# A transformer layer on one core: early maxima in pairs, bias stores spread over chunks, base rows per batch, and another order at the end

## What is computed

```python
B, S, _ = hidden_states.shape
qkv = jnp.transpose((xn @ W_qkv).reshape(B, S, 3, NUM_HEADS, HEAD_DIM), (0, 3, 2, 1, 4))
q, k, v = (qkv[:, :, 0], qkv[:, :, 1], qkv[:, :, 2])
scores = jnp.einsum('bhqd,bhkd->bhqk', q, k) + compute_bias(rel_emb, S, S)
attn = jax.nn.softmax(scores.astype(jnp.float32), axis=-1)
att = jnp.transpose(jnp.einsum('bhqk,bhkd->bhqd', attn, v), (0, 2, 1, 3)).reshape(B, S, EMBED_DIM) @ W_out
...
expert_out = jnp.matmul(jax.nn.gelu(jnp.matmul(xn, w1) + b1), w2) + b2
ffn = expert_out * jnp.sum(combine, axis=-1, keepdims=True)
return x + att + ffn
```

## Time and profile before

| | us |
|---|---|
| median of 3 runs | 3178.73 (3175.87 to 3179.97) |
| the profiled execution | 3177.1 |
| its span, first to last instruction | 3175.2 |
| first pass | 0 to 565 |
| attention, 64 heads | 567 to 3109 |
| projection and stores | 3109 to 3175.2 |

### The profile page before, as it was taken

One profiled execution on the slowest core, in us unless ns is written; L12 is line 12 of the kernel. 1 busy time (PEld: TensorE's weight loads), 2 busy tenths in 40 slices (PEclk: granted clock), 3 DMA queues, 4 the chain that ended last, 5 costly groups with the idle time before them and its releaser, 6 DMA issues.

```text
span 3175.2 us, 72323 instructions
## 1 busy us (share of the span) xinstructions
PE 3137.2 (99%) x28162; PEld 1780.7 (56%) x28162; DVE 2816.9 (89%) x3745; ACT 2437.5 (77%) x4665; POOL 1299.6 (41%) x1920
## 2 busy tenths in 40 slices
PE   7999999999999999999999999999999999999998
PEld 6988889544444444444444444444444444444447
DVE  5577765899999999999999999999999999999923
ACT  4444335688888888888888888888888888888893
POOL 1211212444444444444444444444444444444445
PEclk9999999999999999999999999999999999999999
DMA  8433224432222222222222222222222222222106
GB/s 199 120 93 87 80 80 115 74 68 37 38 38 37 38 38 37 38 38 38 38 37 38 37 38 38 38 38 38 37 38 38 38 38 38 38 38 37 24 9 191
DMA packets 135541, 174.37 MB, mean 55 GB/s; under 512 B 52913, under 2 KB 99633, under 8 KB 128865
## 3 DMA queue, kind: packets, MB, share of 16 engines
q1 hardware_dynamic: 135200, 169.75, 26.2%
HBM read 109.26 MB, written 56.69 MB: 52 GB/s over the span
## 4 chain that ended last, share of the span: by engine, by line
PE 80%; DMA 1%; POOL 0%; DVE 0%; SPq 0%; issue 0%; ACT 0%; DVEq 0%; POOLq 0%; ACTq 0%
PE ps L1153 38%; PE ps L1170 25%; PE ps L1175 9%; PE ps L1142 7%; DMA out_rows<-base_in 1%; PE ps L1209 0%; DVE max_half L1091 0%; DMA base_in<-base_rows 0%; POOL k_st L259 0%; POOL prob L1056 0%; POOL turned L1064 0%; ACT turned L1016 0%; DMA total_sb<-o_sb 0%; DMA recip_rows<-recip_all 0%; SPq L920 0%
## 5 line engine op out<-in xcount | busy, mean ns | idle before, releaser
L1091 DVE TENSOR_REDUCE max_half<-ps 128x1 f32<-128x512 f32 (+1 forms) x2666 | 2408.5, 945 | 35.9 <-PE ps L1142 27.0
L1009 ACT ACTIVATE prob<-ps 128x512 f32<-128x512 f32 x4096 | 2156.4, 600 | 360.2 <-PE ps L1153 356.8
L1056 POOL TENSOR_TENSOR prob<-prob,near 128x224 f32<-128x224 f32 (+2 forms) x1664 | 976.0, 601 | 1384.5 <-ACT prob L1009 1378.1
L1142 PE MATMUL ps<-k_st,q_st 48*128 48x512 f32 x3968 | 1485.5, 461 | 0.4 <-DVE max_half L1091 0.3
L1153 PE MATMUL ps<-q_st,k_st 49*128 49x512 f32 x4096 | 1347.3, 431 | 3.2 <-PEq L266 2.3
L1153 PEld LDWEIGHTS ps<-q_st,k_st 49*128 49x128 f32 x4096 | 661.8, 184 | 864.7 <-ACT prob L1009 728.6
L1170 PE MATMUL ps<-prob,vr 128*32 128x384 f32 x4864 | 757.0, 498 | 0.0
L1142 PEld LDWEIGHTS ps<-k_st,q_st 48*128 48x128 f32 x3968 | 640.7, 184 | 62.1 <-DVE max_half L1091 9.8
L1170 PE MATMUL ps<-prob,vx 128*32 128x384 f32 x3328 | 594.6, 500 | 2.4 <-POOL prob L1056 1.3
L728 PE MATMUL ps<-xnt,w_parts 128*128 128x512 f32 x1152 | 271.7, 395 | 7.7 <-DVE parts L569 4.3
L1175 PE MATMUL ps<-prob,vx 128*32 128x128 f32 x7040 | 276.0, 277 | 0.4 <-POOL prob L1056 0.4
(11 more groups left out here) (70 smaller groups left out, 1162.6 us busy)
## 6 DMA issues: line engine op xcount, KB each, us to landing
qk_parts<-parts SPq DMA_DIRECT2D x64, 512.0 KB, 4.5
q_st<-qk_parts SPq DMA_DIRECT2D x192, 128.0 KB, 3.8
k_st<-qk_parts SPq DMA_DIRECT2D x192, 128.0 KB, 5.5
near<-bias_near SPq DMA_DIRECT2D x64, 352.0 KB, 6.3
x_sb<-in_L_attn_hidden_states SPq DMA_DIRECT2D x16, 512.0 KB, 6.3
base_rows<-x_sb SPq DMA_DIRECT2D x16, 512.0 KB, 2.9
recip_rows<-recip_all SPq DMA_DIRECT2D x256, 32.0 KB, 1.8
base_in<-base_rows SPq DMA_DIRECT2D x16, 512.0 KB, 5.4
```

The lines of the kernel that those rows point to most:

```text
L1009: nc.scalar.activation(prob[:, t % PROBS, CH * j:CH * (j + 1)], ps[:, bank_of(at)], ACT.Exp).then_inc(drained, 1)
L1056: nc.gpsimd.tensor_tensor(at, at, near[n % GROUP][:, side, c0:c0 + q1 - q0], ALU.mult).then_inc(near_done, 1)
L1091: nc.vector.tensor_reduce(max_half[:, m % 2].rearrange("p i c -> p (i c)")[:, k:k + len(banks)], tiles, AX.X, ALU.max) \
L1142: mm = nc.tensor.matmul(ps[:, MAX_BANK + bank], query_block(q_st[u][0:ROWS], k // CPB), k_st[u][0:ROWS, CH * (k % CPB):CH * (k % CPB + 1)] ...
```

## The change

- Early pieces stand in twos at the end of each F2 tile: pieces 2t and 2t + 1 after tile t, none after QK tile 1. Even pieces go to banks 0 and 1, odd ones to banks 4 and 5, and each waits for the maximum of the piece two before it (piece 0 for the low parts of the transposes, piece 1 for GELU). PE's wait for the last maximum of a chunk stands ahead of the next chunk's F1.
- The near tables are stored in 8 transfers of 4 heads and one side each, one in each of chunks 1 to 8, behind the load of x. Before they were two transfers of 16 heads ahead of chunk 0's parts.
- ACT waits for the early maxima ahead of the value copies of the last batch's first chunk, not ahead of that chunk.
- Base rows have a place for each batch: `base_in` for batch 0, the memory of the stacks for 1 and 2, `prob` for 3. SP loads batch 1's when the last scores are made, batch 2's after the last head's reciprocals are spread, batch 3's after chunk 3's store and the last head's `keep`. No load waits for a store. The last chunk is stored in four tiles.
- The high and low parts 0, 1 and 2 are made at the end of heads 32, 33 and 34. The last `collect` comes ahead of the other parts, the last `normalise` ahead of low part 6.

```diff
@@ -59,7 +59,8 @@
-EARLY_QK = 1
+EARLY_BANKS = [0, 4]
+NEAR_STORES = 8
@@ -396,9 +397,12 @@
-                for side in range(2):
-                    sp.dma_start(near_d[:, :, side], bass.AP(tensor=line_d.tensor, offset=P - 1 + side * (LINE + PAD),
-                                                             ap=[[2 * LINE, H], [-1, P], [1, NT]])).then_inc(near_stored, 16)
...
+                def store_near(i):
+                    side, h = i % 2, i // 2 * (2 * H // NEAR_STORES)
+                    sp.dma_start(near_d[h:h + 2 * H // NEAR_STORES, :, side],
+                                 bass.AP(tensor=line_d.tensor, offset=2 * LINE * h + P - 1 + side * (LINE + PAD),
+                                         ap=[[2 * LINE, 2 * H // NEAR_STORES], [-1, P], [1, NT]])).then_inc(near_stored, 16)
@@ -408,6 +412,8 @@
+                    if 0 < CPB * b + c <= NEAR_STORES:
+                        store_near(CPB * b + c - 1)
...
@@ -555,8 +561,9 @@
+                    bank = EARLY_BANKS[piece % 2]
...
-                    nc.vector.tensor_reduce(max_early[:, :, bass.ds(i, 1), j], ps[:, 0:2].unsqueeze(2), AX.X, ALU.max).then_inc(max_done, 1)
+                    nc.vector.tensor_reduce(max_early[:, :, i:i + 1, j], ps[:, bank:bank + 2].unsqueeze(2), AX.X, ALU.max).then_inc(max_done, 1)
...
@@ -598,13 +603,12 @@
-                        if early and t > 0:
-                            early_max(b, c, 2 * t)
...
+                            early_max(b, c, 2 * t)
@@ -681,6 +685,8 @@
+                    if n == CPB * (B - 1):
+                        act.wait_ge(max_done, EARLY)
...
@@ -732,9 +734,15 @@
-                    wait(pe, max_done, early_first(b, c) + piece)
+                    bank = EARLY_BANKS[piece % 2]
+                    if piece >= 2:
+                        wait(pe, max_done, early_first(b, c) + piece - 1)
+                    elif piece == 1:
+                        wait(pe, gelu_done, KF * (CPB * b + c + 1))
+                    else:
+                        wait(pe, xt_low, KE * (CPB * b + c + 2))
...
-                        last = nc.tensor.matmul(ps[:, h], query_block(q_early[HALF * h:HALF * h + ROWS], i),
+                        last = nc.tensor.matmul(ps[:, bank + h], query_block(q_early[HALF * h:HALF * h + ROWS], i),
@@ -752,9 +760,10 @@
-                        if early and m == EARLY_QK:
-                            early_scores(b, c, 0)
...
+                        if f == 0 and b > 0:
...
+                            wait(pe, max_done, min(early_first(b, c), EARLY))
@@ -774,9 +783,6 @@
-                    if early:
...
-                        wait(pe, max_done, early_first(b, c) + 1)
@@ -796,12 +802,8 @@
-                            if early and t > 0 and f == KF // 2 - 1:
-                                early_scores(b, c, 2 * t)
...
-                            if t == 0:
...
-                                wait(pe, xt_low, KE * (n + 2))
+                            early_scores(b, c, 2 * t)
@@ -811,12 +813,12 @@
-                pe.wait_ge(max_done, EARLY)
...
+            base_more = nc.alloc_sbuf_tensor_at("base_more", [P, B - 2, CPB, TPC, E], F32, offset=stack_base)
...
@@ -869,6 +871,16 @@
+            TURN_FROM, NORM_LAST, KEEP_LAST = 2 * H, 2 * TURNED, CPB
...
+            def base_at(i):
...
+                b, c = i // CPB, i % CPB
+                if b == 0:
+                    return base_in[:, c]
+                if b == B - 1:
+                    return prob[:, c, 0:TPC * E].rearrange("p (t e) -> p t e", t=TPC)
+                return base_more[:, b - 1, c]
@@ -945,11 +957,11 @@
-                def load_base(b, c):
...
-                    wait(sp, stored[c], 16 * b)
-                    sp.dma_start(base_in[:, c], base_d[S * b + CH * c:S * b + CH * (c + 1), :].rearrange("(t p) e -> p t e", p=P)) \
-                        .then_inc(rows_in[c], 16)
+                def load_base(b):
...
+                    for c in range(CPB):
+                        sp.dma_start(base_at(CPB * b + c), base_d[S * b + CH * c:S * b + CH * (c + 1), :].rearrange("(t p) e -> p t e", p=P)) \
+                            .then_inc(rows_in[CPB * b + c], 16)
@@ -970,20 +982,26 @@
-                        for c in range(CPB):
-                            load_base(0, c)
+                        load_base(0)
+                sp.wait_ge(score_ready, CPB * KB * NH)
+                load_base(1)
...
-                keep(NH - 1)
-                for b in range(B):
-                    for c in range(CPB):
-                        sp.wait_ge(res_done, TPC * (CPB * b + c + 1))
-                        sp.dma_start(out[S * b + CH * c:S * b + CH * (c + 1), :].rearrange("(t p) e -> p t e", p=P), base_in[:, c]) \
-                            .then_inc(stored[c], 16)
-                        if b + (c > 0) in range(1, B):
-                            load_base(b + (c > 0), (c + CPB - 1) % CPB)
+                load_base(2)
+                for i in range(B * CPB):
+                    if i == KEEP_LAST:
+                        keep(NH - 1)
+                        sp.wait_ge(pv_done, summed(NV * NH - 1))
+                        load_base(B - 1)
+                    if i < B * CPB - 1:
+                        sp.wait_ge(res_done, TPC * (i + 1))
+                        sp.dma_start(out[CH * i:CH * (i + 1), :].rearrange("(t p) e -> p t e", p=P), base_at(i)).then_inc(stored[i % CPB], 16)
+                    else:
+                        for t in range(TPC):
+                            sp.wait_ge(res_done, TPC * i + t + 1)
+                            sp.dma_start(out[CH * i + P * t:CH * i + P * (t + 1), :], base_at(i)[:, t]).then_inc(stored[i % CPB], 16)
...
-                    sp.wait_ge(stored[c], 16 * B)
+                    sp.wait_ge(stored[c], 16 * (B + (TPC - 1 if c == CPB - 1 else 0)))
@@ -1020,10 +1038,10 @@
-                for i in range(TURNED - 1):
-                    high(i)
+                    if 0 <= n - TURN_FROM < TURNED:
+                        high(n - TURN_FROM)
...
-                for i in range(TURNED - 1, B * CPB):
+                for i in range(TURNED, B * CPB):
@@ -1072,10 +1090,11 @@
-                for i in range(TURNED - 1):
-                    low(i)
-                normalise(NH - 1)
-                for i in range(TURNED - 1, B * CPB):
+                    if 0 <= n - TURN_FROM < TURNED:
+                        low(n - TURN_FROM)
+                for i in range(TURNED, B * CPB):
+                    if i == NORM_LAST:
+                        normalise(NH - 1)
@@ -1125,12 +1144,11 @@
-                    b, c = i // CPB, i % CPB
...
-                            dve.wait_ge(rows_in[c], 16 * (b + 1))
-                        nc.vector.tensor_tensor(base_in[:, c, t], base_in[:, c, t], ps[:, PROJ_BANK + t, 0:E], ALU.add).then_inc(res_done, 1)
+                            dve.wait_ge(rows_in[i], 16)
+                        nc.vector.tensor_tensor(base_at(i)[:, t], base_at(i)[:, t], ps[:, PROJ_BANK + t, 0:E], ALU.add).then_inc(res_done, 1)
```

11 lines of the change are left out of this document (3 added, 8 removed).

## The result

| | median us | lowest to highest | ratio to before, 95% interval |
|---|---|---|---|
| before | 3178.73 | 3175.87 to 3179.97 | |
| after | 3145.02 | 3143.23 to 3146.93 | 0.9897 [0.9886, 0.9909] |

What follows compares the result with a forecast made beforehand. PE was taken as busy 99% of the span, with gains in chunk 1, the early chunks and the end; -8.7 - 10.3 - 1.3 + 14 + 1.2 - 14.7 = -19.8 us gave a median of 3159, range 3141 to 3169.

Steps and rivals of the forecast that it cites:

- Term 1: Chunk 1: with the near stores out of chunk 0, its wait goes and it takes 31.0 us; -8.7 us (8.0 to 9.1).
- Term 2: Eight early chunks: pieces in twos cost 1.00 us instead of 1.32; -10.3 us, bounds -13.8 and 0.
- The wait of 1.33: PE's wait ahead of the last batch's first chunk: moved to F1, where the maximum is long done; -1.3 us.
- Term 3: Ahead of chunk 4: a near transfer on four engines delays the early scores' stacks; +14 us (1 to 17).
- L - 2.9 - 0.4: Delay of chunk 4 by a near transfer of length L, less 2.9 us of idle DMA and 0.4 us of margin.
- Term 4: Heads 32 to 34: making the first projection parts there costs ACT and POOL time; +1.2 us (0 to 3).
- Term 5: The end: PE projects without a pause from about 3109, transfers then set the finish; -14.7 us (11 to 17.5).
- PE, ACT and POOL each close behind: Attention stage, 39.7 us a head: said to be paced by DVE, the other three engines nearly as busy.
- adjacency gives nothing: Rival for the early pieces: each pair of matmuls needs its own change, term 2 is 0, time 3169; chance 0.08.
- The end did give back less: Rival: the last head's gather lands late for chunk 12, the end gains 8 and not 14.7, 3166; chance 0.10.
- The slower end: Rival: deeply queued loads and stores fall to 170 GB/s at the end, +18 us, median 3192; chance 0.02.
- The rival of sixteen engines: Near transfers spread over sixteen engines as before: +1 instead of +14 us, giving 3146; chance 0.25.

Runs made afterwards that it cites:

- the variant without DVE's wait: Changed kernel with DVE taking the last head's reciprocals behind the additions of chunks 0 to 2 instead of ahead of them: 3142.89 us.
- the first two variants of the end: Changed kernel with DVE's last reciprocals behind the additions of chunks 0 to 2 (3142.89 us); behind chunk 0's, with totals issued ahead of batch 1's loads (3143.71 us).
- the run with eight in a row: Changed kernel with all eight near stores, cut by heads, ahead of chunk 0's stores instead of one in each of chunks 1 to 8: 3177.18 us.

## Why the prediction was right or wrong

**Term 1** (-8.7) came out to a tenth, with chunk 1 at 31.02 us. The run with all near stores ahead, cut by rows, adds to its reading: they need not have left chunk 0.

**Term 2** (-10.3, bounds -13.8 and 0) was right in its mechanism and too small. The mis-sized number is the second pair of matmuls, which I priced at 0.34 us, "the first step after a change"; it measured 0.91 - 0.66 = 0.25, so the row of 0.23 was the nearer one. With 32 pairs that is 2.8 us. The early chunks of "35.0 us" were 34.66. The wait of 1.33 went as forecast, and DVE kept up.

**Term 3** (+14, bounds 1 and 17) measured +1.5. The choice of four engines, not sixteen, was right; "each with the work of four: L = 16.8" was the step that failed. It took the 131 ns a packet of sixteen engines at work together. Four engines alone take 63 ns (the 4096 packets of after), so their rate is 85 to 100 GB/s, not a quarter of 170, and L about 9 us. By the same formula L - 2.9 - 0.4 that is 5.6 us. The measured 1.5 is lower still. A reading that fits, which no run isolates: the twelve free engines have done their part of the stacks' loads by then, and the four run theirs against little traffic (share 0.19 from 137 to 142, three engines of sixteen). Before, the last of k_early's loads landed 30.6 us after chunk 3's start, now 32.5. The clock granted stayed at 1.00 behind the wait, so the 1.6 us for that were not paid either. I had named "four engines alone meet less traffic" and took only a little off for it.

**Term 4** (+1.2): heads 32 to 34 took 39.66 to 39.67 us where they took 39.64 to 39.76. No cost.

**Term 5** (-14.7, bounds 11 and 17.5) measured -8.9, outside its bounds. The failed step is "PE goes on at about 3109 at full clock": PE needs the addition of chunk 0 to have its banks back for chunk 1, and DVE's program has the last reciprocals ahead of it. The order stood in the code; I placed the reciprocals only on the path of the normalisation and did not ask what is queued behind them on DVE. Before, their totals landed 1.7 us after issue; now they were issued behind 2 MB of loads and took 5 to 6, so DVE stood until 3095. The run with the reciprocals behind the additions shows this cause: the wait goes. PE lost 6.25 us and then 1.8 (45.22 against 43.42 for 360 matmuls): the clock was at 0.5 for 6.8 us, of which PE stood for the first 2.7. That the DMA engines would bound the end was also wrong for this kernel, where PE's last chunk is the last thing but one; the variant without DVE's wait showed that it is the next bound, 3.7 us further down.

**A reading beside the sum.** In the attention "PE, ACT and POOL each close behind" holds for PE alone: from 700 to 800 us of the kernel before PE is busy for 99.59 of 100 us, DVE for 99.27, ACT for 85.47 and POOL for 45.14. No term rests on it.

**Rivals.** That adjacency gives nothing fell. The end did give back less, but not by the gather for chunk 12, for which PE never waited. The slower end fell: with loads and stores queued deep the DMA engines moved 296 GB/s in after (3100 to 3140) and 337 and 351 in the first two variants of the end (3110 to 3135). The rival of sixteen engines fell too, though its time came out: the share was 0.25.

## What to carry over

An engine that waits for one small transfer holds everything that stands behind that wait in its program, and a transfer is late when large loads have been issued ahead of it; so when loads are moved early, follow every small round trip on the same queue, each of its transfers, and put the loads between its steps. Cut a DRAM-to-DRAM copy so that its first dimension stays at sixteen, as the runs cut by rows did. Pieces on halves of the array's rows are cheaper in twos (0.91 us against 1.32), if the second has banks of its own. And a total that comes out can hide two errors: compare the terms, one by one.

## What the runs showed of the hardware

- A transfer whose source and destination begin with a dimension of 4 keeps four of the sixteen DMA engines busy: share 0.25 to 0.27 in after and in the run with eight in a row, 0.95 to 1.0 with a dimension of 16. Eight in a row do not run beside one another (96 GB/s throughout).
- The mean time of a packet of 1408 bytes from DRAM to DRAM differed with the cut of the copy and with what ran beside it: 131 ns in two transfers of 2816 KB on sixteen engines, 91 ns in eight of 704 KB cut by rows, 77 ns where those lie apart, 63 ns on four engines.
- A pair of matmuls on the halves of the rows between full-row matmuls costs 0.66 us, two pairs 0.91. The Trainium skill, TensorEngine Tiling (Array Packing), section "Key Properties", says that a change of the tiling mode drains TensorE; the trace agrees in kind, and the saving of 0.41 us for each place with one change and back fewer gives its size here.
- With one idle time of 1.32 us after each of F2's tiles, the granted clock fell to 0.5 eight times for 3.4 us each in the first three early chunks of the variant with twos on one bank pair, and not in the other five, whose idle times are the same.
- Four transfers of 2 KB landed 5.0 to 6.0 us after their issue behind four of 512 KB, and 1.7 to 1.8 us after it in the kernel before, where they are issued with no load ahead.
